# Moving the making of pair_v to VectorE and all pair-product evictions to ScalarE, with new places for the pair and transpose work, in a fused embedding, pair-interaction and MLP kernel

## The reference

```python
sparse_embed = emb_tables[field_idx[None, :], x_sparse]      # 1024 x 26 x 64
z = sparse_embed.reshape(B, N_FIELDS * K)                    # 1024 x 1664
gram = jnp.einsum('bik,bjk->bij', sparse_embed, sparse_embed)
inner = gram[:, iu, ju]                                      # the 325 pairs i < j
dnn_in = jnp.concatenate([x_dense, z, inner], axis=-1)       # 1024 x 2002
h = jax.nn.relu(dnn_in @ w1 + b1)                            # w1 is 2002 x 2002
out = jax.nn.sigmoid(h @ w2 + b2)
```

## Time and profile before

| | |
|---|---|
| median of 2 runs | 465.27 us (464.39 to 466.15) |
| the profiled execution: its own time | 470.89 us |
| its span, first to last instruction | 469.1 us |
| granted PE clock, mean | 0.967 |
| busy: PE, DVE, ACT, POOL | 419.3, 308.2, 263.9, 257.6 us |
| gathers: number, mean, first issue, last issue | 208, 1105 ns, 3.88 us, 342.06 us |

### The profile page before, as it was taken

One profiled execution on the slowest core, in us unless ns is written; L12 is line 12 of the kernel. 1 busy time (PEld: TensorE's weight loads), 2 busy tenths in 40 slices (PEclk: granted clock), 3 DMA queues, 4 the chain that ended last, 5 costly groups with the idle time before them and its releaser, 6 DMA issues.

```text
span 469.1 us, 6104 instructions
## 1 busy us (share of the span) xinstructions
PE 419.3 (89%) x1969; PEld 343.5 (73%) x1969; DVE 308.2 (66%) x621; ACT 263.9 (56%) x364; POOL 257.6 (55%) x423
## 2 busy tenths in 40 slices
PE   8988589795789988999977999799899999999997
PEld 8766467674668767888856888677678887787885
DVE  4664245641295998486798899775437879887442
ACT  3533055473599496699576676443426967634420
POOL 6777777777777787777787777777720000000000
PEclk9999979989699999999998999999989999899999
DMA  7768466863348868674975774987547433667610
GB/s 240 174 204 217 114 140 152 250 206 67 68 106 194 183 159 241 158 202 81 206 217 115 160 231 77 226 234 243 149 113 240 155 127 121 174 220 243 197 42 1
DMA packets 29456, 77.97 MB, mean 166 GB/s; under 512 B 8480, under 2 KB 8488, under 8 KB 29424
## 3 DMA queue, kind: packets, MB, share of 16 engines
q1 hardware_dynamic: 22768, 70.75, 49.1%
q0 software_dynamic: 6656, 6.83, 12.8%
HBM read 77.55 MB, written 0.00 MB: 165 GB/s over the span
## 4 chain that ended last, share of the span: by engine, by line
PE 44%; POOL 19%; issue 12%; DVE 11%; DMA 6%; another core or an unknown queue 4%; ACT 3%; POOLq 0%; DVEq 0%; ACTq 0%
POOL z L486 18%; PE ps L612 13%; PE ps L600 13%; PE ps L602 12%; PE ps L560 5%; DMA z<-in_L_rec_emb_tables_dram,idx 4%; DVE w_lo L771 3%; POOL pause L493 2%; DVE tail L833 2%; ACT gram L700 2%; DVE gram L805 2%; PE ps L546 1%; DVE weighed L875 1%; ACT w_hi L665 1%
## 5 line engine op out<-in xcount | busy, mean ns | idle before, releaser
L486 POOL DMA_INDIRECT z<-in_L_rec_emb_tables_dram,idx x208 | 229.9, 1105 | 76.1 <-issue 58.0
L600 PE MATMUL ps<-w_hi,x_hi 128*128 128x502 f32 (+1 forms) x512 | 208.4, 407 | 17.9 <-ACT x_hi L673 6.8
L602 PE MATMUL ps<-w_lo,x_hi 128*128 128x502 f32 (+1 forms) x480 | 191.5, 399 | 0.0
L771 DVE TENSOR_TENSOR w_lo<-w_raw,w_hi 128x1002 fp32r<-128x1002 f32 x120 | 141.1, 1201 | 64.8 <-ACT w_hi L665 48.6
L665 ACT CAST w_hi<-w_raw 128x1002 fp32r<-128x1002 f32 x128 | 128.6, 1032 | 66.6 <-DMA w_raw<-in_L_rec_w_dram 39.7
L612 PE MATMUL ps<-w_hi,x_lo 128*128 128x502 f32 (+1 forms) x480 | 143.8, 397 | 4.3 <-DVE x_lo L843 2.5
L600 PEld LDWEIGHTS ps<-w_hi,x_hi 128*128 128x128 f32 x512 | 99.1, 193 | 42.9 <-issue 15.8
L612 PEld LDWEIGHTS ps<-w_hi,x_lo 128*128 128x128 f32 x480 | 91.6, 193 | 24.2 <-DVE x_lo L843 3.3
L602 PEld LDWEIGHTS ps<-w_lo,x_hi 128*128 128x128 f32 x480 | 93.3, 194 | 17.2
L673 ACT CAST x_hi<-ps 128x256 fp32r<-128x256 f32 (+3 forms) x37 | 16.8, 458 | 79.7 <-PE ps L546 54.4
L779 DVE TENSOR_TENSOR x_lo<-ps,x_hi 128x256 fp32r<-128x256 f32 (+3 forms) x37 | 19.4, 530 | 60.4 <-ACT x_hi L673 42.9
(11 more groups left out here) (45 smaller groups left out, 190.3 us busy)
## 6 DMA issues: line engine op xcount, KB each, us to landing
w_raw<-in_L_rec_w_dram SPq DMA_DIRECT2D x112, 501.0 KB
w_raw<-in_L_rec_w_dram SPq DMA_DIRECT2D x24, 250.5 KB
w_raw<-in_L_rec_w_dram SPq DMA_DIRECT2D x8, 438.4 KB
z<-in_L_rec_emb_tables_dram,idx POOLq DMA_INDIRECT x208
w_raw<-in_L_rec_w_dram SPq DMA_DIRECT2D x24, 62.6 KB
w2b<-in_L_rec_w_dram SPq DMA_DIRECT2D x1, 501.0 KB
w2b<-in_L_rec_w_dram SPq DMA_DIRECT2D x1, 500.0 KB
w_raw<-in_L_rec_w_dram SPq DMA_DIRECT2D x8, 50.9 KB
```

What stands on the lines that cost most here:

```text
L486: pool.indirect_dma_start(out=z[:, t % 2, K * f:K * (f + 1)], out_offset=None, in_=emb_rows, in_offset=bass.IndirectOffsetOnAxis(ap=idx[:, ...
L600: nc.tensor.matmul(into(c, t), hi, of_w(w_hi, c, k), start=first, stop=False)
L602: nc.tensor.matmul(into(c, t), hi, of_w(w_lo, c, k), start=False, stop=False)
L771: nc.vector.tensor_tensor(low, raw(n)[at, :], high, ALU.subtract).then_inc(w_lo_done, 1)
```

## The change

For every tile, DVE now makes all of `pair_v`: a new `tensor_scalar` (x_hi times 0.5, into `pair_v[0:K]`) beside the copies of x_lo into `pair_u` and x_hi into `pair_v[K:2K]`. ACT keeps one kind of copy, x_hi into `pair_u[0:K]`, and drops the scaled one (all tiles) and the copy into `pair_v` (tiles 0 to 3). ACT now evicts all four groups of pair products; DVE evicts none. The DVE transpose of `gram` waits for DVE's own earlier tail sums instead of its own evictions. And `PLAN` is another table. The sum of matmuls, transposes, weight splits and gathers is the same.

```diff
     PLAN = {
-        ('O', 0): [15.5, 23.8],
+        ('O', 0): [16.7, 24.3],
...
-        ('T', 7): [73.6, 73.8, 77.5, 80.1],
+        ('T', 7): [70.6, 76.4, 76.5, 80.6],
...
     def by_act(t):
-        return (0, 1, 2) if t < 4 else (0, 2)
+        return (0, 1, 2, 3)
...
-    ACT_COPIES = (0, 1, 2, 3)
...
-                    nc.scalar.copy(pair_u[0:K, :, :, at:at + n, :].rearrange(two), high)
-                    if t in ACT_COPIES:
-                        nc.scalar.copy(pair_v[K:2 * K, :, :, at:at + n, :].rearrange(two), high)
-                    last = nc.scalar.mul(pair_v[0:K, :, :, at:at + n, :].rearrange(two),
-                                         high.bitcast(fp32), 0.5)
+                    last = nc.scalar.copy(pair_u[0:K, :, :, at:at + n, :].rearrange(two), high)
...
-                    for pairs, x in ((pair_u, x_lo), (pair_v, x_hi))[0:1 if t in ACT_COPIES else 2]:
+                    nc.vector.tensor_scalar(
+                        pair_v[0:K, :, :, at:at + n, :].rearrange("p a s f b -> p (a s) f b"),
+                        x_hi[K * par:K * (par + 1), t % XS, first:first + n, :].rearrange(
+                            "p f (g b) -> p g f b", b=2).bitcast(fp32), 0.5, None, ALU.mult)
+                    for pairs, x in ((pair_u, x_lo), (pair_v, x_hi)):
...
                 dve.wait_ge(gram_act, act_banks(t, GBANKS - 1))
-                dve.wait_ge(gram_dve, dve_banks(t, GBANKS - 1))
+                if t >= 1:
+                    dve.wait_ge(tail_done, t)
```

More of the change, by code:

```diff
@@ L137, in product_interaction_mlp_kernel @@
     PLAN = {
-        ('J', 0): [-0.8, 1.0, 2.1, 5.1, 6.1, 8.9, 10.6, 13.1, 14.6, 17.1, 18.6, 20.1, 20.9, 22.4],
-        ('J', 1): [25.3, 25.8, 28.6, 29.9, 33.1, 35.0, 37.4],
-        ('O', 0): [15.5, 23.8],
[L141 to L145, removed]
-        ('R', 1): [33.4],
-        ('X', 1): [35.2],
-        ('O', 2): [35.8, 38.3],
-        ('G', 2): [40.4, 41.0, 41.2, 42.5],
@@ L150, in product_interaction_mlp_kernel @@
[L150 to L154, removed]
-        ('X', 3): [52.2],
[L156 to L169, removed]
-        ('X', 6): [93.5],
-        ('T', 7): [73.6, 73.8, 77.5, 80.1],
[L172 to L175, removed]
+        ('J', 0): [-1.0, 1.0, 2.1, 5.1, 6.1, 8.9, 10.6, 13.1, 14.6, 17.1, 18.7, 20.1, 20.7, 22.2],
+        ('J', 1): [25.4, 25.8, 28.6, 29.9, 33.1, 35.0, 36.0],
@@ new lines, in product_interaction_mlp_kernel @@
+        ('O', 0): [16.7, 24.3],
+        ('G', 0): [24.9, 25.6, 25.8, 26.5],
+        ('R', 0): [29.3],
+        ('X', 0): [30.4],
+        ('O', 1): [26.9, 27.7],
+        ('G', 1): [30.4, 31.6, 31.7, 32.5],
+        ('R', 1): [33.4],
+        ('X', 1): [35.0],
+        ('O', 2): [37.4, 38.8],
+        ('G', 2): [41.1, 41.3, 41.9, 42.7],
+        ('R', 2): [47.2],
+        ('X', 2): [50.3],
+        ('O', 3): [42.0, 45.9],
+        ('G', 3): [48.3, 48.9, 49.5, 49.6],
+        ('R', 3): [49.7],
@@ new lines, in product_interaction_mlp_kernel @@
+        ('X', 3): [52.2],
+        ('T', 4): [51.4, 52.2, 52.3, 54.7],
+        ('O', 4): [52.3, 54.8],
+        ('G', 4): [56.4, 57.0, 57.7, 59.7],
+        ('R', 4): [62.0],
+        ('X', 4): [64.8],
+        ('T', 5): [51.7, 54.7, 55.1, 55.6],
+        ('O', 5): [60.8, 61.4],
+        ('G', 5): [64.3, 64.6, 64.7, 65.7],
+        ('R', 5): [65.7],
+        ('X', 5): [67.4],
+        ('T', 6): [76.8, 78.2, 82.8, 84.6],
+        ('O', 6): [85.1, 85.4],
+        ('G', 6): [88.4, 88.4, 88.6, 88.7],
@@ L176, in product_interaction_mlp_kernel @@
+        ('R', 6): [88.9],
+        ('X', 6): [93.5],
+        ('T', 7): [70.6, 76.4, 76.5, 80.6],
+        ('O', 7): [90.6, 90.9],
+        ('G', 7): [94.3, 95.0, 95.5, 95.6],
+        ('R', 7): [96.0],
+        ('X', 7): [97.2],
     }
```

## The result

The changed kernel takes **487.36 us** (median of 2 runs, 486.05 and 488.66) against 465.27: ratio **1.042, 95% interval 1.034 to 1.050**, slower. The profiled execution took 486.05 us with a span of 484.0, so 14.9 us more span than before; the medians differ by 22.1. Of the 7 us between the two, 5.6 are that the profiled execution before was longer than its two plain runs. 28 more runs of that kernel, made beside the experiments, lie between 464.8 and 473.4 us with a median of 468.8, so the two plain runs stand at its fast end; against 468.8 the changed kernel is 4.0% slower. Where I cut a time into parts, the 14.9 us are meant.

What follows compares the result with a forecast made beforehand. The prediction took GpSimd's self-paced gather stream to bound the kernel, with PE meeting it at T(7,2). Its terms 6.5 + 2.7 + 1.2 + 1.0 = +11.4 us on the median 465.3 gave 476.7 us, range 467 to 488.

Steps and rivals of the forecast that it cites:

- What bounds the kernel: GpSimd's 208 gathers are a self-paced stream that PE, running ahead, meets at fixed times such as T(5,2) and T(7,2).
- ACT's relief is worth nothing: ACT loses 29.5 us net; banks may free sooner around tile 0, but gather batches cap the gain: nothing at the end.
- L784 at 0.645 us: The new scaled-half tensor_scalar on DVE was taken to last 0.645 us, as L792; DVE gains 13 us.
- The gather stream, +6.5 us: Up to T(7,2)'s last gather, 25.8 us of added DVE copying delays gathers by 0.33 per us, less 2.0 for evictions.
- T(7,2) one turn ahead, +2.7: T(7,2) moves ahead of turn 77, leaving one more 2.73 us turn behind it; PE waits there some 5 us.
- Clock, +1.2 behind T(7,2): A 5 us PE wait at T(7,2) is followed by a lower granted clock, costing 1.2 us (0 to 1.5).
- After T(7,2), +1.0: Possible 1 to 2 us wait at G(6,0), two 0.45 us evictor waits, some 0.6 back from tile 7: +1.0 us.
- (a): Rival, 32%: copies hardly hold the gathers, price 0.1 to 0.2 instead of 0.33; 470.8 to 473.4 us.
- (b): Rival, 6%: faster; the stream is so early that PE never waits for it and ACT's relief counts; 456 us.
- (c): Rival, 11%: full block, every DVE copy stops GpSimd for its length; 491.4 us.
- (d): Rival, 11%: DVE bounds; tensor_scalar at 1.08 us, splits 2 to 3 us late at T(5,3) and tile 6; 478 to 484 us.

Runs made afterwards that it cites:

- e5: The kernel before with each of DVE's 48 pair copies made twice, the second time as a copy: 493.5 us, 1.052 times the kernel before.
- e6: The kernel before with each of DVE's 48 pair copies made a second time, as a tensor_tensor maximum: 509.8 us, 1.089 times the kernel before.
- e8: The changed kernel with one pause memset after each fourth gather instead of four: 461.1 us, 0.984 times the kernel before.
- e9: The kernel before with one pause memset after each fourth gather instead of four: 451.1 us, 0.958 times the kernel before.
- e12: The kernel before with only the scaled half of pair_v moved from ACT to DVE: 483.8 us, 1.027 times the kernel before.
- e1: The changed kernel with the old PLAN (table of places), so the split of work alone: 492.3 us, 1.049 times the kernel before.
- e2: The kernel before with the new PLAN (table of places), its split of work unchanged: 476.0 us, 1.018 times the kernel before.
- e3: The changed kernel with the scaled half of pair_v made on ACT again: 478.0 us, 1.020 times the kernel before.
- e11: The changed kernel with the scaled half made by tensor_copy instead of tensor_scalar, factor 0.5 left out: 480.8 us, 1.021 times the kernel before.

## Why the prediction was right, and where it was not

It gave 476.7 us with 467 to 488, slower the likeliest; 487.36 is just inside. The direction holds, and so does what bounds the kernel. The size was too small by half, and of the mechanism the lag of the stream is measured, but that the added copying makes it was only in part shown: e5 and e6, which add the copying alone, speak against it.

**What bounds the kernel**: right, and now shown by e8 and e9. T(5,2) and T(7,2) wait for gathers as said. Missed was J(1,3), where PE stands for 8.82 us. At T(7,2) the bound is a narrow one: PE came there 1.45 us ahead of the gather.

**ACT's relief is worth nothing**: no gain came of its 26.5 us (29.5 were predicted). Whether the relief itself does harm, as in the rival behind e12, is open. e1 is slower than e12, but they differ in the evictor and in the copies.

**L784 at 0.645 us**: measured 0.626 (the middle one of 32). DVE gained 10.0 us, predicted 13.

**The gather stream, +6.5 us**: the term that was mis-sized. It measured 12.6. The amount of added copying was right (25.8 us predicted, 10.2 + 15.0 = 25.2 measured), the price of 0.33 was not: 0.41 and 0.51 by the fit, and 3.3 us remain that the fit gives to nothing. I had taken it mostly from the memsets (13 of them, not twelve, which makes the 0.24 there 0.23), and they stand in a small part of the stream's time. And e5 does not bear out one price for every us of copying. Also wrong was the picture of a delay that adds up copy by copy (6.7 at T(5,3), 6.5 at the last gather): it was 12.65 at gather 80 and stayed. Part of this is the execution before, whose stream was early just there: e2, e3, e5, e6 and e12 are all 5.7 to 6.4 us behind it at gather 80, even e2, which adds no copy; e2 and e3 have 2.4 and 2.0 of it left at the end. The PE wait of 5.8 us that ends at 58.64 is not in them. What couples the two I can only argue: when PE stalls, the splits stop too, and by the table a stream without DVE beside it is quicker; DVE spent 36.1 us on splits up to gather 80 in the kernel before and 39.6 in the changed one.

**T(7,2) one turn ahead, +2.7, with a wait of 5 us**: the wait was 1.45. PE came there at 350.7, not at 342.5: it left T(5,3) at 267.06 instead of 263, and lost clock on the way. Together with the next two terms 4.9 us were predicted; measured are 3.5 - 1.2 = 2.3.

**Clock, +1.2 behind T(7,2)**: wrong place. From 352.17 to 360 the granted clock is 1.00. It fell earlier. The turns from T(5,3) to T(7,2)'s neighbourhood, first the changed kernel, then the kernel before:

```profile
264.00:331.00 67.00, 61.92 (x282) 51.82 (x283) 47.04 (x109) 36.97 (x62) 50.61 (x79) 0.90 0.61 156
```

```profile
251.00:311.00 60.00, 57.34 (x281) 48.00 (x280) 53.11 (x126) 38.50 (x55) 45.15 (x71) 0.97 0.67 162
```

The same 281 or 282 matmuls took 4.6 us more of PE. The 0.90 is two stretches at the lower level, one behind T(5,2) and T(5,3), which wait one after the other, and one at a group of tile 5's pair products, where PE waits 1.66 us for ACT's eviction:

```profile
265.42:272.25 6.83, 5.19 (x14) 4.25 (x15) 2.32 (x3) 1.41 (x3) 4.62 (x9) 0.50 0.56 93
306.38:313.21 6.83, 6.55 (x22) 5.67 (x23) 4.97 (x20) 4.32 (x11) 5.93 (x3) 0.50 0.57 164
```

e2, with the new places alone, waits 3.0 us at T(5,3) and has 0.90 over the 67 us behind it as well, but most of that at the pair products too, where PE waits 0.98 us for ACT's eviction:

```profile
260.38:263.79 3.41, 3.41 (x12) 2.81 (x10) 0.00 (x0) 0.00 (x0) 2.31 (x7) 0.50 0.76 144
297.93:308.17 10.24, 9.40 (x32) 7.86 (x32) 7.88 (x24) 5.28 (x10) 8.53 (x9) 0.50 0.76 192
```

The kernel before has its one low stretch there, 3.41 us, behind T(5,2). That is the nearest that I come to the 1.8% of the places: this price is in rows, but no run moved T(5,3) or the groups of tile 5 alone.

**After T(7,2), +1.0**: the wait at G(6,0) didn't come, since the new places put the whole run ahead of it; G(6,2) waits 0.62 for its evictor, near the 0.45 that was said. What I didn't see is what the places were worth there: 10.6 us against the old ones (12.6 in e1, 2.0 now).

**The rivals.** (a), a low price: its 470.8 to 473.4 us are refuted for the move, by the result, e3 and e12; that copying by itself is cheap is not refuted, and e5 speaks for it. (b), faster, needed a stream that is early; e8 and e9 make it so, and the change is then still 2.7% slower (0.984 / 0.958). (c), the full block with 491.4, was nearer to the timed 487.4 than the forecast was: the memsets are blocked much as it says, the stream by about half, if the fit's prices are taken. (d)'s event, DVE late with pair operands, came in e1, e5 and e6, not in the changed kernel, and by another cause: not a slow tensor_scalar, but the length of the run in places with three turns of room.

**Open**: how much of the lag is DVE's added work and how much ACT's relief, what the places cost beyond the clock between T(5,3) and T(7,2), and e11's timed ratio.

## What to carry to other kernels

An engine with idle time is not free when it shares something with an engine that paces the program: cost each instruction you move by what it takes from the neighbour per us, and get that price from the rows by sorting the neighbour's instructions by what ran beside them, all kinds, not only the suspected one. Then test the price by adding the work alone, and before a late stream is called held back, look for what it waits. A table of places and a split belong together: test each alone, because here the two costs were not the whole and one paid part of the other back. When two variants of a kernel differ through a stream that bounds both, loosen the stream itself first; here one constant was worth more (4.2%) than the whole question.

## What was not expected of the hardware

- A tensor_tensor on DVE with both inputs in SBUF lengthens an indirect gather of GpSimd: 0.948 us alone, 1.254 beside a weight split (708 gathers), up to 4.06; it leaves a one-column memset alone (0.104 against 0.103).
- A pair copy does the reverse: 0.504 instead of 0.103 on the memset (the scaled half among them), 1.049 instead of 0.948 on a gather.
- DVE's instructions that read PSUM touch neither (0.944 and 0.104).
- A short wait can cost a longer stretch at the lower clock than a long one: in e2 waits of 0.98 us at 297.92 and 0.84 at 304.2 lay in 10.24 us at 0.50, while one of 3.0 us at 258.93 stood ahead of 3.41 us at 0.50.
